# Reordering the end of a mixture-of-experts tail: sixteen small dense blocks, the last expert, and one instruction of each finish

## Chip, cores and metric

The kernel runs on one core of a Trainium2 chip. The metric is device time in microseconds (us), the median of several runs of one whole launch. Engines are named as in the profile: PE (TensorE matmuls), PEld (its weight loads), DVE (VectorE), ACT (ScalarE), POOL (GpSimd), SP (SyncE, which only starts DMAs here).

## What is computed

The input is x of shape (4, 32, 32, 64): four images of 1024 tokens with 64 channels. A Mamba-like mixer (convolution, selective scan, projection) with a residual comes first, then a layer norm and a top-1 mixture of experts:

```
logits = h @ gate_w + gate_b;  probs = softmax(logits);  idx = argmax(probs)
pos  = rank of the token within its expert;  kept = pos < C      # C = 640 slots an expert, 8 experts
buf[idx, pos] = h                                                 # dropped where not kept
hmid = relu(buf @ w1[e] + b1[e]);  ybuf = hmid @ w2[e] + b2[e]    # 64 -> 256 -> 64
y    = nan_to_num(ybuf[idx, pos] * prb * kept, nan=0, posinf=1e4, neginf=-1e4)
out  = t + y                                                      # t: the residual
```

## The kernel before

The program writes out each engine's order of work by hand; engines meet through semaphores. The first three quarters are the mixer: per image and state a scan on DVE, with ACT, POOL and PE around it. The experts come at the end, and the change is there.

**Slots.** All tokens but the last 256 are scattered by their slot number to a table in DRAM (`slots`, eight experts of 640 rows, 5 tiles of 128). The table is read back, one load an expert (`xe[e]`), and worked in 16 chunks: `CHUNKS` holds for each expert a chunk of 3 tiles (384 rows) and one of 2 tiles (256 rows). For chunk i, PE does `turn(i)` (transposes, L1142), ACT `channels(i)` (copy, L878), PE `up(i)` (two matmuls 64 to 256, L1153), ACT `hidden(i)` (two ReLUs, L886 and L888). When both chunks of an expert are there PE does `down` (20 matmul passes for 5 tiles, L1167). `FINISH` lists nine finishes, two for expert 0 and one for each other; so `down(8)` and `finish(8)` are those of the last expert, e=7. `finish(i)` runs on DVE (L1495 to L1509): add the bias, multiply by the gate, replace non-finite numbers, add the residual. POOL then scatters the expert's five tiles to the output rows, one indirect DMA a tile (L615).

**The last 256 tokens** (`LT = 2` tiles) have no time to go through the table. They are computed densely, through all eight experts, with a selector row that shuts the wrong ones: 16 blocks j of half an expert each: PE `dense_up(j)` (L1184), ACT `dense_hidden(j)` (L895), PE `dense_down(j)` (L1196), which all add up in one PSUM bank. Their finish on DVE (L1522 to L1530) is followed by one direct DMA from SP (L454).

**Order at the end.** `BEHIND = 8`: behind each of the last eight chunks PE does one `dense_up` and the `dense_down` of the block before; then `down(8)`; then the other eight blocks in a row:

```
if i >= BEHIND:
    dense_up(i - BEHIND)
...
down(E)
for j in range(len(CHUNKS) - BEHIND, BLOCKS):
    dense_up(j)
    dense_down(j - 1)
dense_down(BLOCKS - 1)
```

On DVE the dense finish comes last, behind `finish(8)`. ACT follows PE's order. POOL ends with `finish(8)`'s five DMAs and a wait for all output scatters; SP ends with the dense tokens' DMA and a wait for it.

Of the kernel before, what the change touches and what calls it, by code (L numbers as in the profile page):

```python
# [5 lines left out]
ALU = mybir.AluOpType  # L6
# [7 lines left out]
B, H, W, C = 4, 32, 32, 64  # L14
# [14 lines left out]
CHUNKS = [(e, k0, k1) for e in range(E) for k0, k1 in ((0, 3), (3, ET))]  # L29
BLOCKS = 2 * E  # L30
FINISH = [(0, 0, 3), (0, 3, ET)] + [(e, 0, ET) for e in range(1, E)]
BEHIND = 8
BAR = 2.0 ** 100
R_RES, R_PRB, R_ID, ROW = C, 2 * C, 2 * C + 1, 2 * C + 2
LT = 2
LW = LT * P
UNITS = [(b, 0, T) for b in range(B - 1)] + [(B - 1, 0, T - LT), (B - 1, T - LT, LT)]
V = len(UNITS)
# [24 lines left out]
def metaformer_layer(nc, x, ln_g, ln_b, in_proj_w, conv_w, conv_b, x_proj_w, dt_proj_w, dt_proj_b, A_log,  # L63
# [7 lines left out]
    with ExitStack() as ctx:  # L71
        def sb(name, shape, dt=F32):
            return ctx.enter_context(nc.sbuf_tensor(name, shape, dt))
# [8 lines left out]
        M0 = ctx.enter_context(nc.psum_tensor("M0", [P, HALF], F32))  # L82
# [77 lines left out]
        bs = sb("bs", [P, 25, T])  # L160
# [18 lines left out]
        def within(buf, start, *dims):  # L179
            size = 1  # L180
            for d in dims:
                size *= d
            flat = buf[:, :, :].rearrange("p a l -> p (a l)")[:, start:start + size]
            names = "abcd"[:len(dims)]
            if len(dims) == 1:
                return flat
            return flat.rearrange(f"p ({' '.join(names)}) -> p {' '.join(names)}",
                                  **{k: d for k, d in zip(names[1:], dims[1:])})
# [10 lines left out]
        ye = within(dA, 0, 4, ET, C)  # L199
# [3 lines left out]
        dy = within(bsb, 2 * L + HALF, 4, LT, C)  # L203
        dout = within(bsb, 3 * L, LT, C)
        dfin = within(bsb, 3 * L + HALF, LT, C).bitcast(I32)

        def four(buf):
# [33 lines left out]
             "b_lgt b_h3 b_ld b_ex b_oh b_base b_acc b_pos b_prb b_ids b_idx b_dve b_dve2 b_dve3 b_res b_sent").split())  # L241

        fill_done, w1_zero, bars = sem("fill_done"), sem("w1_zero"), sem("bars")
        b_hx, d_tr, d_xT, d_up, d_hid, d_dn, d_dve, d_diff, d_fin, d_out = map(
            sem, "b_hx d_tr d_xT d_up d_hid d_dn d_dve d_diff d_fin d_out".split())
        e_in = [sem(f"e_in{e}") for e in range(E)]
        e_out = [sem(f"e_out{i}") for i in range(2)]
        e_zero, e_tr, e_xT, e_up, e_h0, e_h1, e_dn, e_y, e_yo, e_dve, e_diff = map(sem, (
            "e_zero e_tr e_xT e_up e_h0 e_h1 e_dn e_y e_yo e_dve e_diff").split())

        def at(buf, b):

# [9 lines left out]
        def over(col, n):  # L262

            return col.unsqueeze(2).broadcast_to([P, col.shape[1], n])
# [76 lines left out]
        def rows(v):  # L341

            return rows_[:, v % 2]
# [9 lines left out]
        def tiles(psum, n, k=T):  # L353
            return psum.rearrange("p (t c) -> p t c", t=k)[:, :, 0:n]
# [268 lines left out]
        def _(act):  # L623
# [267 lines left out]
            def dense_hidden(j):  # L891
                act.wait_ge(d_up, j + 1)
                if j >= 2:
                    act.wait_ge(d_dn, j - 1)
                ac.activation(hid[:, j % 2, :], Yp[:, j % 2 * HALF:j % 2 * HALF + LW], ACT.Relu,  # L895
                              bias=b1c[:, j:j + 1]).then_inc(d_hid, 1)
# [6 lines left out]
            for i in range(len(CHUNKS)):  # L903
                if 2 <= i + 1 < len(CHUNKS):
                    channels(i + 1)
                hidden(i)
                if i == BEHIND - 1:
                    act.wait_ge(d_tr, 1)
                    ac.activation(hxT[0:HX, :], Yp[0:HX, HALF:HALF + LW], ACT.Copy).then_inc(d_xT, 1)
                if i >= BEHIND:  # L910
                    dense_hidden(i - BEHIND)
            for j in range(len(CHUNKS) - BEHIND, BLOCKS):
                dense_hidden(j)


        @block.tensor
        def _(pe):
# [260 lines left out]
            def dense_up(j):  # L1178
                e, part = j // 2, j % 2
                if j < 2:  # L1180
                    pe.wait_ge(d_xT, 1)
                else:
                    pe.wait_ge(d_hid, j - 1)
                te_.matmul(Yp[:, j % 2 * HALF:j % 2 * HALF + LW], w1s[0:HX, e, part * P:(part + 1) * P], hxT[0:HX, :], start=True,  # L1184
                           stop=True).then_inc(d_up, 1)

            def dense_down(j):
                e, part = j // 2, j % 2
                if j == 0:
                    pe.wait_ge(b_idx, V)  # L1190
                    for t in range(LT):
                        te_.matmul(M0[:, t * C:(t + 1) * C], hxT[0:HX, t * P:(t + 1) * P], b2z[0:HX, :], start=(t == 0),
                                   stop=False, skip_group_check=True)
                pe.wait_ge(d_hid, j + 1)
                for t in range(LT):
                    ins = te_.matmul(M0[:, t * C:(t + 1) * C], hid[:, j % 2, t * P:(t + 1) * P], w2s[:, e, part, :],  # L1196
                                     start=False, stop=(j == BLOCKS - 1 and t == LT - 1), skip_group_check=True)
                ins.then_inc(d_dn, 1)
# [38 lines left out]
            for i in range(len(CHUNKS)):  # L1237
                if i + 1 < len(CHUNKS):
                    turn(i + 1)
                if i == 1:  # L1240
                    down(0)
                up(i)
                if i == 0:
                    back(LAST, 15)
                if i == 1:
                    down(1)
                if i >= 4 and i % 2 == 0:
                    down(i // 2)
                if i == BEHIND - 1:
                    dense_turn()  # L1250
                if i >= BEHIND:
                    dense_up(i - BEHIND)
                if i >= BEHIND + 1:
                    dense_down(i - BEHIND - 1)
            down(E)
            for j in range(len(CHUNKS) - BEHIND, BLOCKS):
                dense_up(j)
                dense_down(j - 1)
            dense_down(BLOCKS - 1)


        @block.vector
        def _(dve):
            ve = nc.vector
# [223 lines left out]
            def finish(i):  # L1488
                e, k0, k1 = FINISH[i]
                m = k1 - k0  # L1490
                link = Chain(dve, e_dve, i, 4)
                y, cl, ok, diff = (ye[:, x, k0:k1] for x in range(4))
                inf = fin[:, k0:k1, :]
                dve.wait_ge(e_dn, i + 1)
                ve.tensor_tensor(y, tiles(turned_down(i), C, m),  # L1495
                                 b2s[:, e, :].unsqueeze(1).broadcast_to([P, m, C]), ALU.add).then_inc(e_y, 1)
                dve.wait_ge(e_y, i + 1)
                link(ve.tensor_tensor(y, y, xe[e][:, k0:k1, R_PRB:R_PRB + 1].broadcast_to([P, m, C]), ALU.mult))

                ve.tensor_tensor(diff, y, y, ALU.subtract).then_inc(e_diff, 1)  # L1500
                ve.tensor_scalar(cl, y, 1e4, -1e4, ALU.min, ALU.max)
                link(ve.tensor_tensor(ok, y, y, ALU.is_equal))
                dve.wait_ge(e_diff, i + 1)
                ve.tensor_scalar(inf, diff, 0.0, None, ALU.is_equal)
                link(ve.tensor_tensor(cl, cl, ok, ALU.mult))
                link(ve.copy_predicated(cl, inf, y))
                if e >= 2:
                    dve.wait_ge(e_out[e % 2], 16 * ET * (e // 2))
                ve.tensor_tensor(yo[:, e % 2, k0:k1], cl, xe[e][:, k0:k1, R_RES:R_RES + C], ALU.add).then_inc(e_yo, 1)  # L1509
                link.end()  # L1510

            finish(0)
            back(LAST, 15)
            for i in range(1, len(FINISH)):
                finish(i)

            link = Chain(dve, d_dve, 0, 4)
            y, cl, ok, diff = (dy[:, i] for i in range(4))
            nt = LT
            dve.wait_ge(d_dn, BLOCKS)  # L1520
            dve.wait_ge(b_idx, V)
            link(ve.tensor_tensor(y, tiles(M0[:, 0:nt * C], C, nt), over(bs[:, 23, 0:nt], C), ALU.mult))  # L1522
            ve.tensor_tensor(diff, y, y, ALU.subtract).then_inc(d_diff, 1)
            ve.tensor_scalar(cl, y, 1e4, -1e4, ALU.min, ALU.max)
            link(ve.tensor_tensor(ok, y, y, ALU.is_equal))
            dve.wait_ge(d_diff, 1)
            ve.tensor_scalar(dfin[:, :, :], diff, 0.0, None, ALU.is_equal)
            link(ve.tensor_tensor(cl, cl, ok, ALU.mult))
            link(ve.copy_predicated(cl, dfin[:, :, :], y))
            ve.tensor_tensor(dout[:, :, :], cl, rows(V - 1)[:, 0:nt, R_RES:R_RES + C], ALU.add).then_inc(d_fin, 1)  # L1530
            link.end()


# [27 lines left out]
```

## Time and profile before

| what | value |
|---|---|
| timed runs | 387.02, 388.14, 391.14 us; median 388.14 us |
| profiled execution, first to last instruction | 397.8 us |
| mean granted TensorE clock of the profiled execution | 0.868 |
| busy share of the span: PE, DVE, POOL, ACT | 79%, 78%, 71%, 59% |

The timed runs and the profiled execution are different executions. No total time of the profiled one stands beside its span; the span alone is 9.7 us longer than the median of the timed runs. A granted clock of 1.00 is 2.4 GHz, 0.50 is 1.2 GHz.

### The profile page before, as it was taken

How to read it: one execution, taken by the hardware profiler on the slowest of the kernel's cores; microseconds unless marked ns; L12 is line 12 of the kernel's file. 1: busy time of each engine (PE TensorE's matmuls, PEld its weight loads, DVE VectorE, ACT ScalarE, POOL GpSimd, SP SyncE). 2: the span in 40 equal slices, each digit the busy share in tenths (PEclk: the TensorE clock that was granted, in tenths of full speed). 3: DMA queues.
4: the chain of work that ended last, by engine and by line, in shares of the span. 5: the costliest groups of instructions: out<-in, count | busy, mean ns of one | idle time of the engine just before them, and what ended most of it. 6: DMA issues, size and time to landing. Idle time of an engine off the chain costs nothing. (4 is left out here: it accounts for less than half of the span.)

```text
span 397.8 us, 4347 instructions
## 1 busy us (share of the span) xinstructions
PE 316.1 (79%) x1257; PEld 188.4 (47%) x1257; DVE 310.1 (78%) x360; ACT 233.3 (59%) x519; POOL 282.1 (71%) x201
## 2 busy tenths in 40 slices
PE   7832986957989896897989698796895798869784
PEld 3311432313535352553545265363773576748764
DVE  4799987999999999987999989999981157425441
ACT  4456797524798984659797268775651455234221
POOL 3435846987993999999599999966877044745760
PEclk9965897999998998879899898989987599968955
DMA  4287999999798699856878769997210900000000
GB/s 99 36 281 248 274 243 366 390 200 368 315 315 323 208 308 297 284 190 244 303 254 298 203 175 325 318 369 226 61 30 19 250 23 4 18 8 17 16 1 8
DMA packets 43986, 78.68 MB, mean 198 GB/s; under 512 B 16050, under 2 KB 26093, under 8 KB 43962
## 3 DMA queue, kind: packets, MB, share of 16 engines
q1 hardware_dynamic: 41066, 73.88, 57.5%
q0 software_dynamic: 2896, 4.53, 4.2%
q8 instruction: 10, 0.16, 0.2%
q14 instruction: 14, 0.11, 0.1%
HBM read 72.30 MB, written 7.54 MB: 201 GB/s over the span
## 5 line engine op out<-in xcount | busy, mean ns | idle before, releaser
L518 POOL TENSOR_TENSOR prod<-h,csb 128x1024 f32<-128x1024 f32 (+1 forms) x64 | 143.7, 2253 | 24.9 <-DMA csb<-bc_rows 10.5
L984 PE MATMUL Yp<-prod,ident 128*128 128x512 f32 (+1 forms) x256 | 124.9, 624 | 13.8 <-POOL prod L518 13.6
L1318 DVE TENSOR_TENSOR_SCAN h<-dA,Bp 128x1024 f32<-128x1024 f32 (+2 forms) x58 | 119.7, 2064 | 4.7 <-DVE Bp L1277 1.0
L984 PEld LDWEIGHTS Yp<-prod,ident 128*128 128x128 f32 x256 | 50.3, 208 | 75.3 <-issue 50.3
L697 ACT ACTIVATE dA<-delta,aneg 128x1024 f32<-128x1024 f32 (+1 forms) x58 | 62.9, 1093 | 23.1 <-DVE h L1318 19.0
L1277 DVE TENSOR_TENSOR Bp<-Cp,bsb 128x1024 f32<-128x1024 f32 (+1 forms) x58 | 67.7, 1168 | 6.4 <-DMA bsb<-bc_rows 4.2
L615 POOL DMA_INDIRECT out_dram<-dA,csb x30 | 30.3, 1009 | 36.5 <-DVE dA L1509 28.9
L558 POOL DMA_INDIRECT slots<-rows_,slot x30 | 30.1, 1002 | 6.9 <-issue 4.5
L1495 DVE TENSOR_TENSOR dA<-Bp,b2s 128x320 f32<-128x320 f32 (+1 forms) x8 | 3.8, 475 | 33.8 <-PE Bp L1167 15.6
L1153 PE MATMUL Cp<-prod,w1s 128*128 128x384 f32 (+1 forms) x64 | 24.7, 508 | 2.0 <-issue 2.0
L895 ACT ACTIVATE bsb<-Yp,b1c 128x256 f32<-128x256 f32 x16 | 7.6, 475 | 23.4 <-PE Yp L1184 14.0
L1167 PEld LDWEIGHTS Bp<-w2s,prod 128*128 128x128 f32 x152 | 18.5, 195 | 2.3 <-issue 1.0
L1167 PE MATMUL Bp<-w2s,prod 128*128 128x64 f32 x152 | 18.3, 276 | 0.2 <-ACT prod L888 0.2
L1196 PEld LDWEIGHTS M<-w2s,bsb 128*128 128x128 f32 x64 | 13.6, 269 | 7.3 <-issue 5.7
L1196 PE MATMUL M<-w2s,bsb 128*128 128x64 f32 x64 | 12.9, 344 | 4.8 <-issue 4.8
L1153 PEld LDWEIGHTS Cp<-prod,w1s 128*128 128x128 f32 x64 | 12.1, 216 | 7.4 <-issue 5.4
L878 ACT ACTIVATE prod<-Bp 64x384 f32<-64x384 f32 (+1 forms) x16 | 6.8, 427 | 14.8 <-PE Bp L1142 7.6
L1184 PE MATMUL Yp<-hxT,w1s 72*128 72x256 f32 x32 | 13.7, 519 | 0.6 <-issue 0.6
L567 POOL TENSOR_TENSOR bsb<-te,bsb 128x1024 f32<-128x1024 f32 (+1 forms) x6 | 13.1, 2179 | 1.2 <-DMA bsb<-bc_rows 1.1
L615 POOL DMA_INDIRECT out_dram<-dA,bsb x10 | 10.1, 1013 | 4.7 <-issue 2.9
L526 POOL TENSOR_TENSOR trel<-trel,ex 128x1024 f32<-128x1024 f32 x3 | 7.1, 2359 | 8.7 <-DVE h L1318 4.9
L886 ACT ACTIVATE prod<-Cp,b1c 128x384 f32<-128x384 f32 (+1 forms) x16 | 8.4, 525 | 7.9 <-PE Cp L1153 5.8
(290 smaller groups left out, 604.8 us busy)
## 6 DMA issues: line engine op xcount, KB each, us to landing
bsb<-bc_rows SPq DMA_DIRECT2D x48, 512.0 KB, 6.7
csb<-bc_rows SPq DMA_DIRECT2D x48, 512.0 KB
bsb<-bc_rows SPq DMA_DIRECT2D x16, 384.0 KB, 5.7
csb<-bc_rows SPq DMA_DIRECT2D x16, 384.0 KB
slots<-fill POOLq DMA_DIRECT2D x1, 2600.0 KB
csb<-slots SPq DMA_DIRECT2D x6, 325.0 KB, 5.3
bcs<-bc_rows SPq DMA_DIRECT2D x2, 512.0 KB, 10.9
xs_in<-in_x_dram SPq DMA_DIRECT2D x1, 768.0 KB, 5.8
```

What stands on the lines that cost most here:

```text
L518: po.tensor_tensor(prod[:, k % 4, c], h[:, k % 3, c], csb[:, k % CSLOTS, c], ALU.mult).then_inc(s_pP, 1)
L558: po.indirect_dma_start(slots_dram[:, :], bass.IndirectOffsetOnAxis(ap=slot[:, v % 2, t:t + 1], axis=0), rows(v)[:, t, :], None, bounds_ch ...
L567: po.tensor_tensor(row, te[:, c], row, ALU.mult).then_inc(p_bx, 1)
L615: po.indirect_dma_start(out_rows, bass.IndirectOffsetOnAxis(ap=xe[e][:, k, R_ID:R_ID + 1].bitcast(I32), axis=0), yo[:, e % 2, k, :], None, ...
L697: ac.activation(dA[:, k % 3, c], at(delta, UNITS[v][0])[:, c], ACT.Exp, scale=aneg[:, n:n + 1]).then_inc(s_dA, 2 if (v, n - 1) in POOLED e ...
L984: ins = te_.matmul(Yp[:, c], idn, prod[:, k % 4, c], start=False, stop=(n == 15), skip_group_check=True)
L1153: te_.matmul(Cp[:, k * HALF:k * HALF + (k1 - k0) * P], w1s[:, e, k * P:(k + 1) * P], xT[:, e % 2, k0 * P:k1 * P], start=True, stop=True).t ...
L1167: ins = te_.matmul(turned_down(i)[:, (k - k0) * C:(k - k0 + 1) * C], part[:, e % 2, k * P:(k + 1) * P], w2s[:, e, x, :], start=(x == 0), s ...
L1184: te_.matmul(Yp[:, j % 2 * HALF:j % 2 * HALF + LW], w1s[0:HX, e, part * P:(part + 1) * P], hxT[0:HX, :], start=True, stop=True).then_inc(d ...
L1196: ins = te_.matmul(M0[:, t * C:(t + 1) * C], hid[:, j % 2, t * P:(t + 1) * P], w2s[:, e, part, :], start=False, stop=(j == BLOCKS - 1 and ...
L1277: ve.tensor_tensor(Bp[:, span(v)], Cp[:, span(v)], bsb[:, k % CSLOTS, span(v)], ALU.mult).then_inc(s_mul, 2 if (v, n - 1) in POOLED else 1)
L1318: ins = ve.tensor_tensor_scan(h[:, k % 3, c], decays, drives, h[:, k % 3, c.start - 1:c.start] if i else 0.0, ALU.mult, ALU.add)
```

## The change

Three edits. First, PE does two dense blocks behind each of the last eight chunks, so all sixteen lie in the loop, and `dense_down(15)` and then `down(8)` come last; ACT's order follows. Second, DVE does the dense finish ahead of `finish(8)`, which is now its last work. Third, in both finishes the test for finite numbers is one instruction, `(y * 0) == 0`, in place of a subtraction `y - y` and a comparison with 0 that waited for it; the semaphores of that wait go.

```diff
 # ACT
                 if i >= BEHIND:
-                    dense_hidden(i - BEHIND)
-            for j in range(len(CHUNKS) - BEHIND, BLOCKS):
-                dense_hidden(j)
+                    dense_hidden(2 * (i - BEHIND))
+                    dense_hidden(2 * (i - BEHIND) + 1)
 # PE
                 if i >= BEHIND:
-                    dense_up(i - BEHIND)
-                if i >= BEHIND + 1:
-                    dense_down(i - BEHIND - 1)
+                    j = 2 * (i - BEHIND)
+                    dense_up(j)
+                    if j:
+                        dense_down(j - 1)
+                    dense_up(j + 1)
+                    dense_down(j)
+            dense_down(BLOCKS - 1)
             down(E)
-            for j in range(len(CHUNKS) - BEHIND, BLOCKS):
-                dense_up(j)
-                dense_down(j - 1)
-            dense_down(BLOCKS - 1)
 # DVE, finish(i); the dense finish likewise, now a function finish_dense()
-                ve.tensor_tensor(diff, y, y, ALU.subtract).then_inc(e_diff, 1)
+                ve.tensor_scalar(inf, y, 0.0, 0.0, ALU.mult, ALU.is_equal)
                 ve.tensor_scalar(cl, y, 1e4, -1e4, ALU.min, ALU.max)
                 link(ve.tensor_tensor(ok, y, y, ALU.is_equal))
-                dve.wait_ge(e_diff, i + 1)
-                ve.tensor_scalar(inf, diff, 0.0, None, ALU.is_equal)
                 link(ve.tensor_tensor(cl, cl, ok, ALU.mult))
 # DVE, order
-            for i in range(1, len(FINISH)):
+            for i in range(1, len(FINISH) - 1):
                 finish(i)
+            finish_dense()
+            finish(len(FINISH) - 1)
```

## Rows read from the trace of the kernel before

**Rows 1.** Stretches of 10 us: busy PE, PEld, DVE, ACT, POOL, granted clock, DMA
```profile
340.00:350.00 10.00, 7.90 (x51) 6.54 (x49) 4.08 (x9) 2.51 (x6) 7.56 (x9) 1.00 0.06 21
360.00:370.00 10.00, 10.00 (x70) 8.91 (x70) 4.25 (x10) 4.26 (x9) 7.01 (x7) 0.95 0.05 18
380.00:390.00 10.00, 8.55 (x31) 7.33 (x30) 2.00 (x5) 2.85 (x6) 5.94 (x6) 0.50 0.02 1
```

**Rows 2.** Chain of waits, last expert at full clock (start, us, what)
```profile
362.97 0.49 PE Yp L1184 x2
...
369.56 0.49 PE Yp L1184 x2
370.04 0.39 PE M L1196 x4
...
371.36 0.43 PE Yp L1184 x2
```

**Rows 3.** Chain of waits, dense blocks behind the last expert
```profile
374.42 0.49 PE Yp L1184 x2
...
375.78 2.65 issue
...
380.51 1.45 issue
...
388.19 0.96 PE Yp L1184 x2
389.15 0.75 PE M L1196 x4
...
390.86 1.69 PE M L1196 x8
```

**Rows 4.** Timeline: dense finish on DVE, first and last, and its DMA
```profile
392.57 0.29 DVE L1522 TENSOR_TENSOR bsb<-M,bs 128x128 f32<-128x128 f32 x1 [10.47 <-PE M L1196]
...
394.36 0.29 DVE L1530 TENSOR_TENSOR bsb<-bsb,rows_ 128x128 f32<-128x128 f32 x1
394.67 0.38 SPq L454 DMA_DIRECT2D out_dram<-bsb  x1
```

**Rows 5.** Timeline: finish of expert 6 on DVE
```profile
369.59 0.49 DVE L1495 TENSOR_TENSOR dA<-Bp,b2s 128x320 f32<-128x320 f32 x1 [2.57 <-PE Bp L1167]
...
370.64 0.49 DVE L1500 TENSOR_TENSOR dA<-dA 128x320 f32<-128x320 f32 x1
...
371.06 0.55 DVE L1501 TENSOR_SCALAR dA<-dA 128x320 f32<-128x320 f32 x1
...
371.53 0.47 DVE L1502 TENSOR_TENSOR dA<-dA 128x320 f32<-128x320 f32 x1
...
372.04 0.33 DVE L1504 TENSOR_SCALAR dA<-dA 128x320 int32<-128x320 f32 x1
372.28 0.48 DVE L1505 TENSOR_TENSOR dA<-dA 128x320 f32<-128x320 f32 x1
...
373.35 0.49 DVE L1509 TENSOR_TENSOR dA<-dA,bsb 128x320 f32<-128x320 f32 x1
```

**Rows 6.** Timeline: POOL's DMAs of experts 6 and 7, first and last of five
```profile
374.63 0.97 POOL L615 DMA_INDIRECT out_dram<-dA,bsb  x1 [0.50 <-issue]
...
380.03 1.09 POOL L615 DMA_INDIRECT out_dram<-dA,bsb  x1 [0.30 <-issue]
...
382.90 0.97 POOL L615 DMA_INDIRECT out_dram<-dA,bsb  x1 [1.78 <-DVE dA L1509]
...
388.00 0.97 POOL L615 DMA_INDIRECT out_dram<-dA,bsb  x1 [0.30 <-issue]
```

**Rows 7.** Chain of waits: an indirect DMA of POOL, from issue to landing
```profile
306.38 2.19 DMA slots<-rows_,slot
```

**Rows 8.** Timeline: work that waited for PE in two stretches
```profile
345.43 2.34 PE L1167 MATMUL Bp<-w2s,prod 128*128 128x64 f32 x20
...
355.63 0.49 DVE L1495 TENSOR_TENSOR dA<-Bp,b2s 128x320 f32<-128x320 f32 x1 [10.84 <-remote]
...
377.86 0.49 DVE L1495 TENSOR_TENSOR dA<-Bp,b2s 128x320 f32<-128x320 f32 x1 [4.02 <-remote]
377.90 0.47 ACT L895 ACTIVATE bsb<-Yp,b1c 128x256 f32<-128x256 f32 x1 [5.60 <-issue]
```

**Rows 9.** Stretches of 2 us, columns as in rows 1
```profile
376.00:378.00 2.00, 0.00 (x0) 0.00 (x0) 0.14 (x1) 0.10 (x1) 1.70 (x2) 1.00 0.06 18
378.00:380.00 2.00, 1.57 (x6) 1.35 (x6) 1.93 (x5) 0.38 (x1) 1.42 (x2) 0.51 0.01 0
...
386.00:388.00 2.00, 2.00 (x10) 1.82 (x9) 0.00 (x0) 0.72 (x2) 1.39 (x2) 0.50 0.01 0
```

More of the change, by code:

```diff
@@ L243, in metaformer_layer @@
         fill_done, w1_zero, bars = sem("fill_done"), sem("w1_zero"), sem("bars")
-        b_hx, d_tr, d_xT, d_up, d_hid, d_dn, d_dve, d_diff, d_fin, d_out = map(
-            sem, "b_hx d_tr d_xT d_up d_hid d_dn d_dve d_diff d_fin d_out".split())
+        b_hx, d_tr, d_xT, d_up, d_hid, d_dn, d_dve, d_fin, d_out = map(
+            sem, "b_hx d_tr d_xT d_up d_hid d_dn d_dve d_fin d_out".split())
         e_in = [sem(f"e_in{e}") for e in range(E)]
         e_out = [sem(f"e_out{i}") for i in range(2)]
-        e_zero, e_tr, e_xT, e_up, e_h0, e_h1, e_dn, e_y, e_yo, e_dve, e_diff = map(sem, (
-            "e_zero e_tr e_xT e_up e_h0 e_h1 e_dn e_y e_yo e_dve e_diff").split())
+        e_zero, e_tr, e_xT, e_up, e_h0, e_h1, e_dn, e_y, e_yo, e_dve = map(sem, (
+            "e_zero e_tr e_xT e_up e_h0 e_h1 e_dn e_y e_yo e_dve").split())
         def at(buf, b):
@@ L1491, in finish @@
                 link = Chain(dve, e_dve, i, 4)
-                y, cl, ok, diff = (ye[:, x, k0:k1] for x in range(4))
+                y, cl, ok = (ye[:, x, k0:k1] for x in range(3))
                 inf = fin[:, k0:k1, :]
@@ L1510, in finish, with finish_dense @@
                 link.end()
+            def finish_dense():
+                link = Chain(dve, d_dve, 0, 4)
+                y, cl, ok = (dy[:, i] for i in range(3))
+                nt = LT
+                dve.wait_ge(d_dn, BLOCKS)
+                dve.wait_ge(b_idx, V)
+                link(ve.tensor_tensor(y, tiles(M0[:, 0:nt * C], C, nt), over(bs[:, 23, 0:nt], C), ALU.mult))
+                ve.tensor_scalar(dfin[:, :, :], y, 0.0, 0.0, ALU.mult, ALU.is_equal)
+                ve.tensor_scalar(cl, y, 1e4, -1e4, ALU.min, ALU.max)
+                link(ve.tensor_tensor(ok, y, y, ALU.is_equal))
+                link(ve.tensor_tensor(cl, cl, ok, ALU.mult))
+                link(ve.copy_predicated(cl, dfin[:, :, :], y))
+                ve.tensor_tensor(dout[:, :, :], cl, rows(V - 1)[:, 0:nt, R_RES:R_RES + C], ALU.add).then_inc(d_fin, 1)
+                link.end()
             finish(0)
             back(LAST, 15)
-            for i in range(1, len(FINISH)):
+            for i in range(1, len(FINISH) - 1):
                 finish(i)
[L1517 to L1531, printed above, removed]
+            finish_dense()
+            finish(len(FINISH) - 1)
 _INS = ['x', 'L0_conv_ln_g', 'L0_conv_ln_b', 'L0_conv_in_proj_w', 'L0_conv_conv_w', 'L0_conv_conv_b',
```

## Prediction

> **What bounds the kernel now.** I read the table of stretches first, since the change touches only the last 60 us, then the chain of waits through the end, and then the timeline of each engine that finishes something there. In the table the reader is to see that PE limits the stage where the slot experts and the dense blocks are mixed: from 360 to 370 it is busy for 10.00 of 10.00 us while DVE, ACT and POOL have room [rows 1]. The chain agrees: from the end of `down(6)` to the end of `down(7)`, 362.97 to 369.56, it stays on PE throughout, 6.59 us for an expert with two dense blocks [rows 2]. Behind `down(8)`, which ends at 374.42, the chain is still PE's: eight dense ups and nine downs until 392.55, 18.13 us, of which 4.10 (2.65 and 1.45) are waiting without a visible cause and the rest is work, most of it at the half clock [rows 3]. Then come the dense finish and its DMA: 392.57 to 394.67 on DVE, and from there to the end of the span at 397.8 another 3.13 [rows 4]. In all, 23.4 us from the end of `down(8)` to the end.
>
> A second way ends beside it and is almost hidden in this trace: `finish(8)` on DVE and POOL's five indirect DMAs, the last issued at 388.00 [rows 6]. With about 2.2 us to land [rows 7] that was done near 390.2, some 7 us ahead of the dense way. So the question is which of the two ways is the longer one when the dense blocks run faster than here.
>
> **The profiled execution and the timed ones.** The span is 397.8 us and the median of the timed runs 388.14, so the profiled execution lost at least 9.7 us that the timed runs did not lose. I looked in the chain for losses that no instruction explains, and found two stretches where signals from PE come late. PE's record of `down(5)` ends at 345.43 + 2.34 = 347.77, but DVE, which waits for it, starts at 355.63; `down(6)` ends 15.2 us after `down(5)` where 6.59 is the pace, so this stretch cost 8.6 us. In the second, DVE's `finish(8)` starts at 377.86 and ACT's next dense ReLU at 377.90, though PE put half a microsecond of work between the two signals [rows 3, 8]: two signals that should lie 0.49 apart arrive 0.04 apart, as if they had been held back together. PE had then nothing to do from 376 to 378, and its granted clock fell from 1.00 to 0.51 in the next 2 us [rows 9]. Without the late signal I see no reason for the fall. I take it that the timed runs have neither, in the main; that is the choice on which the forecast hangs, and the rivals are its other outcomes.
>
> The Trainium skill has two rules that bear on it, and the sum below doesn't use them. TensorE: Matmul & The Clock Gate (Part 1) says that the half clock is the state of rest and that sustained activity releases it; by that a tail of back-to-back dense blocks would run at the full clock, as I take it, though the trace speaks against it for a while: PE is busy for 2.00 of 2.00 us from 386 to 388 at a granted 0.50 [rows 9]. Runtime: NRT & Kernel Launch (The launch sequence) gives 9 to 15 us around the instructions of a kernel; if the timed runs hold that, their span would be an estimated 373 to 379 us, and more than the 9.7 us of late signals and half clock would be missing from them; no run here shows it.
>
> **The change, part by part.** All times from D, the end of `down(8)` in the old order, at the full clock and without late signals.
>
> Before, dense way: 8 ups at 0.43 to 0.49 and 9 downs at 0.39 make 3.7 + 3.5 = 7.2 us [rows 2], then 392.55 to 397.8, 5.25 [rows 4]: D + 12.5. At the half clock the ups cost 0.96 and the downs 0.75, 14.4 us [rows 3]: D + 19.7.
>
> Before, POOL way: it starts with expert 6. `down(7)` ends 4.86 us ahead of D (369.56, 374.42). `finish(7)` runs from 369.59 to 373.84, 4.25 us, and POOL's first DMA comes 0.79 later, at 374.63 [rows 5, 6]; that is 5.07 behind `down(7)`. Its five DMAs hold POOL from 374.63 to 381.12, 6.49; then 0.3 of issue, and expert 7's five, 382.90 to 388.97, 6.07. Expert 7's result is ready sooner (4.86 + 5.07 = 9.93 behind `down(7)`) than POOL is free (11.9). The last DMA lands 2.19 after its issue, 1.22 after the end of its record, and the close of the program takes about 0.4 (the span's end less 394.67 and the direct DMA's median of 2.7). Sum: 5.07 + 6.49 + 0.3 + 6.07 + 1.22 + 0.4 = 19.55 behind `down(7)`, or D + 14.7. This is longer than the dense way's 12.5: where PE is not slowed, the end of the kernel before is POOL's.
>
> After, PE: the eight blocks move ahead of `down(8)`. They fill no hole, since PE had none in that stage at the full clock [rows 1, 2]; the stage gets longer by what they cost, and `down(8)` ends at D + 7.2. In the loop the order up(j), down(j-1), up(j+1), down(j) leaves 0.39 + 0.43 = 0.8 us between an up and the down that needs its ReLU of 0.47 [rows 2, 8], so I charge nothing for waits; behind `hidden` of the same chunk ACT is some 0.6 us late, and if that cover went the cost would be up to 0.3 a chunk, 2.4 in all (the upper bound).
>
> After, DVE: `finish_dense` is queued ahead of `finish(8)`. It waits for `dense_down(15)`, which ends a `down` (2.2 us) before `finish(8)` can start, and takes about 2.1 less one instruction [rows 4]: covered. SP's DMA of the dense tokens goes out sooner and is off the path; nothing else is queued on SP. POOL is free again: `finish(7)` is now some 7 us ahead of `finish(8)` and not 4.9.
>
> The shorter finish: the steps from L1500 to L1505 took 372.28 - 370.64 = 1.64 us for four instructions. Three are left, of which the new two-operation one is bounded by the starts of its kind: 0.24 (L1504 to L1505) and 0.47 (L1501 to L1502) [rows 5]. So 0.2 to 0.4 us is saved in each finish; I take 0.2, since the new one has two operations as L1501. Only the last one lies on the path; the others are covered by PE's 6.6 to 8.3 us an expert.
>
> After, the end: behind `down(8)` come `finish(8)` 0.03 + 4.05, the step to POOL 0.79, five DMAs 6.07, landing 1.22, close 0.4: 12.6 us, with no way round it. End: D + 7.2 + 12.6 = D + 19.8.
>
> **Sum.** +5.1 us against D + 14.7: 388.14 + 5.1 = 393.2 us. What is moved behind the common PE work is the longer finish (12.6 us against the dense 5.25), and the POOL time that used to run beside the dense blocks now has nothing beside it. Bounds of this case: POOL's five at 6.07 or 6.49, the saved 0.2 or 0.4, PE's waits 0 to 2.4, and POOL's lag before: 3.9 to 7.5, or 392 to 395.6.
>
> Against the profiled execution the same end would be 374.42 + 19.8 = 394.2, 3.6 us shorter than 397.8, because that one paid 4.1 of late signals and 7 of half clock behind D.
>
> **Rivals.** *The tail of the timed runs is at the half clock, without late signals* (chance 0.20). For it: the clock did not come back in 18 us of dense blocks [rows 3, 9]. Then before ends at D + 19.7 by the dense way, and after, whose blocks lie among chunks that ran at 1.00, at D + 19.8: 388.2.
>
> *The timed runs are like the profiled one and the new order mends it* (0.17), the case on the other side: before ends at D + 23.4, and PE, with two blocks and the next chunk at hand, bridges the late signals; after at D + 19.8 is 3.6 us faster, 384.5, and if it bridges part of the first stretch's 8.6 too, down to 380. It decides from the point where late signals and half clock cost the timed tail more than 5.1 us. Against it: 9.7 us of span that the timed runs don't have.
>
> *The new loop itself is slowed* (0.10): four dense blocks an expert with more hand-overs between PE and ACT bring a wait that drops the clock. One expert with four blocks takes 6.59 + 2 x 0.85 = 8.3 us at the full clock and twice that at half; one such expert gives +8.3: 401.5.
>
> *The change does nothing* (0.03): the end of the timed runs is set by something that neither order moves: 388.
>
> **How the numbers follow.** The first case has 0.50. Runs of one kernel here differ by 1% (387.02 to 391.14), so within 1% means 384.3 to 392.0. Slower by over 1%: 0.43 of the first case and 0.10 of the slowed loop, 0.53. Within 1%: 0.07 of the first, 0.20, 0.03 and a little of the third, 0.32 together. Faster by over 1%: 0.15 from the third. The range runs from 384.3 to 397: below it some 0.1 of the third case is left out, above it the slowed loop.
>
> **What will show it.** Right: in the profile of the changed kernel the chain ends with `down`'s L1167, the DVE finish, five POOL DMAs at L615 and a landing, about 12.6 us behind the last matmul; SP's dense DMA lands more than 8 us before the end; an expert with four dense blocks takes about 8.3 us at full clock, with PE busy all the time. Wrong: gaps of PE in the last eight chunks that the second block fills (an expert with four blocks at less than 7.5 us), or a timed gain, which would say that the timed runs before had the half clock or the late signals behind `down(8)`; or DVE's L1495 starting well behind the last L1167.

## Result and profile after

The changed kernel takes 390.63 us (median of 20 runs, 387.46 to 398.71), the kernel before 388.79 us (20 runs, 384.58 to 395.87). Their ratio is 1.0071, 95% interval 1.0038 to 1.0104: 1.5 to 4.0 us slower, 2.8 at the middle. Some executions of either kernel take some per cent longer at a lower granted clock; the ratios leave them out and the medians do not, so a ratio is not the quotient of two medians. The profiled execution of the changed kernel took 393.05 us, 1.85 us more than its span of 391.2; so a time and a span differ by little here.

The chain of waits at the end of the changed kernel (start, us, what):

```profile
369.27 0.50 PE Yp L1183 x2
...
370.98 2.25 PE Bp L1166 x20
...
373.25 0.50 DVE dA L1494
...
376.37 0.50 DVE dA L1506
...
382.77 0.97 POOL out_dram L615
```

The way is the one that was forecast: the last down of PE, the last finish on DVE, five DMAs of POOL. The last matmul ends at 373.23, and 18.0 us follow, against the 5.25 that followed the last matmul in the first profile of the kernel before [rows 4]. The five-us stretches of the same kernel (columns as in rows 1) show the stage itself:

```profile
345.00:350.00 5.00, 5.00 (x37) 4.42 (x37) 0.86 (x2) 2.42 (x5) 3.78 (x5) 1.00 0.09 30
360.00:365.00 5.00, 5.00 (x35) 4.30 (x34) 1.01 (x2) 3.33 (x8) 3.48 (x4) 1.00 0.07 23
365.00:370.00 5.00, 5.00 (x35) 4.62 (x34) 3.44 (x8) 2.49 (x6) 2.41 (x3) 1.00 0.05 12
```

PE is busy throughout at the full clock; an expert with four dense blocks takes 8.35 us (the dense ups behind one expert's down start at 349.07, 357.42 and 365.77 in the chain). But POOL, busy 3.78 us of 5 when it issues one DMA after the other, falls to 2.41: it runs dry. Its timeline in the changed kernel, the first DMAs of experts 5, 6 and 7 and the last of all:

```profile
361.87 0.97 POOL L615 DMA_INDIRECT out_dram<-dA,csb  x1 [0.91 <-DVE dA L1506]
...
370.21 0.97 POOL L615 DMA_INDIRECT out_dram<-dA,bsb  x1 [2.19 <-DVE dA L1506]
...
377.66 0.97 POOL L615 DMA_INDIRECT out_dram<-dA,bsb  x1 [1.02 <-DVE dA L1506]
...
382.77 0.97 POOL L615 DMA_INDIRECT out_dram<-dA,bsb  x1 [0.31 <-issue]
```

The brackets give POOL's idle time ahead of each DMA. The comparison is with a second profile of the kernel before, which the first experiment brought (span 382.6; its own time 384.30). It has no late signals and no half clock in this stage, and is called undisturbed below:

```profile
329.72 0.97 POOL L615 DMA_INDIRECT out_dram<-dA,csb  x1 [4.15 <-DVE dA L1509]
...
357.40 2.40 PE L1167 MATMUL Bp<-w2s,prod 128*128 128x64 f32 x20
...
362.52 1.09 POOL L615 DMA_INDIRECT out_dram<-dA,bsb  x1 [0.31 <-issue]
...
367.00 0.66 PE L1196 MATMUL M<-w2s,bsb 128*128 128x64 f32 x4 [0.17 <-ACT bsb L895]
...
369.03 0.97 POOL L615 DMA_INDIRECT out_dram<-dA,bsb  x1 [0.30 <-issue]
...
369.81 0.38 SPq L454 DMA_DIRECT2D out_dram<-bsb  x1
...
374.13 0.97 POOL L615 DMA_INDIRECT out_dram<-dA,bsb  x1 [0.30 <-issue]
```

From expert 1's first DMA at 329.72 on, POOL never waits for DVE again: 35 DMAs, 0.30 apart. The last `down` ends at 359.80, the last matmul at 367.66, the dense tokens' DMA starts at 369.81, and POOL is busy with its DMAs until 375.10. So before, POOL's queue was the end of the kernel, and PE's dense blocks ran beside it at no cost. In this profile 14.9 us follow the last matmul. The spans of the two profiles differ by 8.6 us, but 5.2 of these lie ahead of expert 1's first DMA (329.72, 334.93), where PE's order is the same in both.

In both kernels 7.5 us follow POOL's last record (375.10 to 382.6, 383.74 to 391.2). The trace holds what fills it, though the views leave it out: the landing, and then a drain record on POOL of 5.88 us, from 376.47 in the kernel before and 385.13 in the changed one.

### The profile page after: what moved, and what is told of

It reads as the page before. It is cut to its first block and busy times, and to the rows that moved or that the text cites. A ratio compares the mean times of both kernels' runs of the same rounds, so it can differ in the third digit from the quotient of the medians.

```text
span 391.2 us, 4327 instructions
## 1 busy us (share of the span) xinstructions
PE 305.6 (78%) x1257; PEld 182.0 (47%) x1257; DVE 308.7 (79%) x350; ACT 233.8 (60%) x519; POOL 280.9 (72%) x201
## 5 line engine op out<-in xcount | busy, mean ns | idle before, releaser
L615 POOL DMA_INDIRECT out_dram<-dA,csb x30 | 30.0, 1001 | 28.2 <-DVE dA L1506 20.6
L558 POOL DMA_INDIRECT slots<-rows_,slot x30 | 30.1, 1004 | 6.4 <-issue 5.1
L1152 PE MATMUL Cp<-prod,w1s 128*128 128x384 f32 (+1 forms) x64 | 21.4, 458 | 0.0
L707 ACT ACTIVATE Bp<-delta,aneg 128x512 f32<-128x512 f32 (+1 forms) x12 | 7.8, 652 | 8.4 <-DVE h L1317 8.2
L962 PE MATMUL M<-u,wdt 128*128 128x512 f32 x12 | 8.4, 793 | 4.4 <-ACT u L647 3.2
L691 ACT ACTIVATE Cp<-te 128x1024 f32<-128x1024 f32 x3 | 3.1, 1029 | 14.0 <-DVE Bp L1276 14.0
L1296 DVE TENSOR_TENSOR_SCAN h<-dA,hl,Bp 128x256 f32<-128x256 f32 x16 | 11.0, 731 | 0.3
```

The lines of the kernel that those rows point to most:

```text
L558: po.indirect_dma_start(slots_dram[:, :], bass.IndirectOffsetOnAxis(ap=slot[:, v % 2, t:t + 1], axis=0), rows(v)[:, t, :], None, bounds_ch ...
L615: po.indirect_dma_start(out_rows, bass.IndirectOffsetOnAxis(ap=xe[e][:, k, R_ID:R_ID + 1].bitcast(I32), axis=0), yo[:, e % 2, k, :], None, ...
L1152: te_.matmul(Cp[:, k * HALF:k * HALF + (k1 - k0) * P], w1s[:, e, k * P:(k + 1) * P], xT[:, e % 2, k0 * P:k1 * P], start=True, stop=True).t ...
L1296: ve.tensor_tensor_scan(h[:, ring(q), w], dA[:, ring(q), w], Bp[:, w], hl[:, n:n + 1], ALU.mult, ALU.add).then_inc(s_scan, 1)
```

## Experiments

The theory, call it A: POOL's 35 DMAs from expert 1 to the end take about 45 us without a gap, plus 7.5; the kernel's end moves by the gaps that an order of PE leaves in that queue, and by nothing else. Rivals: the loss lies in PE's longer loop, in the clock, in the new finish, or the kernel before lost time in a slow dense tail. Whole times of one kernel scatter by some per cent, and much of that arises ahead of the stage changed here: in the twelve later profiles POOL's first DMA of expert 0 starts anywhere from 319.5 to 324.9. So beside each ratio stands the *tail*: from POOL's first DMA of expert 1 to the end of the span, in the one profile of each kernel, and POOL's idle time in it beyond the 0.31 between two DMAs. Each ratio is against the kernel before in the same rounds.

| kernel | ratio to before (95%) | tail, us | POOL idle, us |
|---|---|---|---|
| before, again | 1.0011 (0.9962 to 1.0060) | 52.86 | 0.0 |
| changed | 1.0071 (1.0038 to 1.0104) | 56.31 | 3.2 |
| order alone | 1.0118 (1.0036 to 1.0200) | 56.29 | 4.0 |
| finish alone | 1.0052 (1.0001 to 1.0103) | 53.40 | 0.0 |
| all blocks last | 0.9982 (0.9942 to 1.0022) | 53.03 | 0.0 |
| twelve in the loop | 1.0030 (0.9992 to 1.0068) | 53.84 | 1.3 |
| changed, last expert in two | 1.0071 (1.0031 to 1.0111) | 55.32 | 2.5 |
| changed, SP waits | 1.0067 (1.0022 to 1.0111) | 54.91 | 2.8 |
| before, SP waits | 0.9953 (0.9912 to 0.9994) | 51.49 | 0.0 |
| before, finish and SP waits | 0.9979 (0.9945 to 1.0014) | 52.03 | 0.0 |
| before, by chunks | 0.9850 (0.9779 to 0.9921) | 51.13 | 0.0 |

**Before, again** (no edit).

> The kernel before, unchanged, for a second profile. Theory A (the late signals and the half clock of the first profile are not the rule): the span is 385 to 388 us, no wait of DVE for PE behind a finished down is longer than 2 us, and POOL's last DMA and the drain behind it (5.9 us in both profiles) end within 2 us of the dense tokens' DMA. Rival R (they are the rule): two late stretches again, 8 and 4 us, and the end 23 us behind the last expert's down, by the dense way alone.

The late signals did not come again and the clock was full until the last matmul, as A expected; the span, 382.6, was 2.4 us under the range named. The dense tokens' DMA and POOL's end were not within 2 us of each other: that DMA started 5.3 us ahead of the end of POOL's last DMA and 12.5 ahead of the end of the drain, so POOL's way was the longer one by more than expected.

**Order alone and finish alone.** The changed kernel with the old finish, and the kernel before with the new one (both edits as in the diff above).

> The order of after with the old finish. Theory A: the order carries the whole loss, 0.2 to 0.6 us above after, ratio to before 1.007 to 1.010. Rival (the new finish costs, the order is free): the time of before, ratio 1.000.

> The order of before, only the finish with one instruction less. Theory A: 0.2 to 0.6 us less, ratio 0.998 to 1.000, since one finish at most lies on the path. Rival (DVE's finishes pace the last experts): eight finishes at 0.4 to 0.6 us, 3 to 5 us less, ratio 0.988 to 0.992.

The order carries the loss: its tail is the changed kernel's (56.29 and 56.31), and not 0.2 to 0.6 us above it as expected. Its gaps are 0.8 us longer than the changed kernel's, but its 35 DMAs hold POOL 0.7 us less (34.4 and 35.2). So A's "by nothing else" holds to about half a microsecond: in the kernels of the table the 35 DMAs take between 34.4 and 35.6 us of POOL's time. The finish alone gains nothing; its interval lies at or above 1, and its tail is 0.54 longer although POOL has no gap. The cost is in POOL's DMAs themselves, summed over experts 0 to 5 and 6 to 7; first before, then with the new finish (busy, mean ns):

```profile
L615 POOL DMA_INDIRECT out_dram<-dA,csb x30 | 30.0, 1001 | 28.0 <-DVE dA L1509 19.8 <-issue 8.2
L615 POOL DMA_INDIRECT out_dram<-dA,bsb x10 | 9.8, 984 | 3.0 <-issue 3.0
```

```profile
L615 POOL DMA_INDIRECT out_dram<-dA,csb x30 | 30.5, 1017 | 27.7 <-DVE dA L1507 20.7 <-issue 7.0
L615 POOL DMA_INDIRECT out_dram<-dA,bsb x10 | 9.9, 990 | 3.0 <-issue 3.0
```

The same 0.5 us lies between the two kernels with SP's wait (51.49 and 52.03). The expected small gain did not come; what came is a loss of that size, in one profile of each.

**Without the last expert's DMAs** (changed kernel; 640 rows of the output are not written).

```diff
-                for k in range(k0, k1):
+                for k in range(k0, k1 if e < E - 1 else k0):
...
-                pool.wait_ge(e_out[i], 16 * ET * len(range(i, E, 2)))
+                pool.wait_ge(e_out[i], 16 * ET * len(range(i, E - 1, 2)))
```

> After, without the last expert's five output DMAs (its 640 rows are not written). Theory A (the end is POOL's way: five DMAs, a landing, then a drain of 5.9 us): the drain starts behind expert 6's landing, so the end comes some 7 us sooner, span near 384. Rival (the drain or the end waits for PE, DVE or SP): less than 2 us, or, if the drain shrinks when little is outstanding, 13 us or more.

The span is 383.7, 7.5 us less than the changed kernel's, though PE and DVE end where they did (373.17 and 376.81, there 373.22 and 376.87). POOL's five DMAs are the end, not the finish. This is one execution, without a ratio. The drain took 5.47 us with five DMAs fewer, 0.41 less. Two values don't tell how much of it is fixed: at 0.08 us a DMA, an estimate from these two, the 40 output DMAs would make 3.3 of the 5.88, and with the 30 that POOL issues to fill the table (L558) nearly all of it.

**Where the wait stands.** The wait for the output's landing goes from POOL to SP, in the kernel before and in the changed one.

```diff
 # POOL
-            for i in range(2):
-                pool.wait_ge(e_out[i], 16 * ET * len(range(i, E, 2)))
 # SP, at its end
+            for i in range(2):
+                sp.wait_ge(e_out[i], 16 * ET * len(range(i, E, 2)))
```

> The order and the finish of before; only the wait for the output DMAs' landing goes from POOL to SP, so POOL's drain can start at once behind its last DMA. Theory A (POOL's way ends the kernel, and the drain is a fixed 5.5 to 5.9 us that needn't wait for the landing): 1.2 us less in the end, ratio 0.997. Rival (the drain waits for the landing itself, or the dense way is the end): no change; the drain is 1.2 us longer.

> After, with the same one edit. Theory A: 1.2 us less than after, ratio to before 1.004 to 1.006. Rival: as after, 1.007.

Both tails are 1.4 us shorter (52.86 to 51.49, 56.31 to 54.91), and POOL's last record now lies 6.1 us ahead of the end in place of 7.5: the landing goes on beside the drain. That the same edit is worth the same in both shows that POOL's way ends both kernels. The ratio of the kernel before (0.9953) agrees; that of the changed one (1.0067 beside 1.0071, where 1.004 to 1.006 was expected) is too coarse to show it.

**Last expert in two parts** (changed kernel).

```diff
-FINISH = [(0, 0, 3), (0, 3, ET)] + [(e, 0, ET) for e in range(1, E)]
+FINISH = [(0, 0, 3), (0, 3, ET)] + [(e, 0, ET) for e in range(1, E - 1)] + [(E - 1, 0, 3), (E - 1, 3, ET)]
...
-                done = i + 1 if i < 2 else 2 * e + 2
+                done = 2 * e + (1 if k1 == 3 else 2)
...
                     if j:
                         dense_down(j - 1)
+                    if i == len(CHUNKS) - 1:
+                        down(E)
                     dense_up(j + 1)
...
-            down(E)
+            down(E + 1)
```

> After, with the last expert finished in two parts: three tiles in the middle of the last chunk, two at the very end. Theory A (the loss is POOL standing idle while PE does the dense blocks ahead of the last down): POOL starts on the last expert sooner and has only two DMAs behind the last down, so 3 to 4.5 us come back, ratio to before 0.997 to 1.002, the gaps between POOL's experts but the last two unchanged. Rival (the loss is in PE's longer loop or in the clock): as after, 1.007, or worse for a finish more on DVE.

POOL's timeline in it, the first DMAs of experts 5 and 6, the first of expert 7 and the last:

```profile
361.77 0.97 POOL L615 DMA_INDIRECT out_dram<-dA,csb  x1 [0.92 <-DVE dA L1508]
...
370.10 0.97 POOL L615 DMA_INDIRECT out_dram<-dA,bsb  x1 [2.18 <-DVE dA L1508]
...
376.57 0.97 POOL L615 DMA_INDIRECT out_dram<-dA,bsb  x1 [0.30 <-issue]
...
381.67 0.97 POOL L615 DMA_INDIRECT out_dram<-dA,bsb  x1 [0.30 <-issue]
```

The tail fell by 1.0 us, not by 3 to 4.5. The number was worked out against A's own rule: POOL is held by expert 6's DMAs until 376.3 whenever they started at 370.1, so only the last gap of 1.02, less the 0.31 of issue, could go. The gaps at 361.77 and 370.10 are as in the changed kernel, as A wants. The ratio is too coarse to tell 1 us.

**All blocks last, and twelve in the loop.** In the kernel before, `BEHIND = 16` puts all sixteen dense blocks behind the last expert; the other edit puts two blocks behind each of chunks 8 to 11, one behind each of 12 to 15, four behind the last expert.

> Before, with all sixteen dense blocks behind the last expert and none in the loop. Theory A (POOL paces the end, PE's order is free as long as POOL is fed): POOL has no gap from the second expert on, the end is POOL's drain, the time of before to 0.5%. Rival (the dense blocks alone at the end run at the half clock and end last): sixteen blocks at 1.7 us, PE's last matmul some 10 us later than in the second profile of before, the end 5 to 8 us later.

> The finish and the DVE order of before; twelve dense blocks in the loop, two behind each of chunks 8 to 11 and one behind each of the last four, four behind the last expert. Theory A (an expert with four dense blocks takes PE 8.35 us and POOL 6.4, so each lets POOL run dry by up to 2 us once its queue is used up): of two such experts the queue of 3 to 4 us covers nearly all, POOL's gaps together 0 to 1 us, ratio 1.000 to 1.003. Rival (any block ahead of the last down costs its 0.85 us): 3.4 us later, ratio 1.009.

With all blocks last PE ends later against POOL's queue, and nothing is lost: no gap, a tail of 53.03. These blocks, 14 us of dense work in a row, ran at the full clock (five-us stretches of that kernel):

```profile
360.00:365.00 5.00, 5.00 (x37) 4.58 (x36) 2.45 (x7) 2.69 (x6) 3.78 (x4) 1.00 0.06 19
365.00:370.00 5.00, 5.00 (x36) 4.49 (x36) 0.49 (x1) 2.56 (x7) 3.78 (x5) 1.00 0.03 7
```

That ends the rival of a dense tail at the half clock for the executions that were profiled. Here the queue even holds DVE back: the last expert's finish waits 4.25 us for expert 5's rows to land before it may write over them in one of the two output buffers:

```profile
366.81 0.49 DVE L1510 TENSOR_TENSOR dA<-dA,bsb 128x320 f32<-128x320 f32 x1 [4.25 <-DMA out_dram<-dA,csb]
```

With twelve in the loop there is one large gap in the queue beyond expert 1, where the pairs have used it up, and a small one of 0.50 ahead of expert 6:

```profile
361.93 0.97 POOL L616 DMA_INDIRECT out_dram<-dA,csb  x1 [1.43 <-DVE dA L1510]
```

Idle 1.3 us, a little over the 0 to 1 expected; the tail is 1.0 longer than before's. The rival's 0.85 us for each block moved would have given 3.4. So 0, 8, 12 and 16 blocks ahead of the last down, all with the old finish, give tails of 53.0, 52.9, 53.8 and 56.3: no price until POOL's queue is empty.

**Before, with the new finish and SP's wait; then by chunks.** If POOL's queue is the end, it ends sooner when it is fed sooner. So every chunk gets a down and a finish of its own:

```diff
-FINISH = [(0, 0, 3), (0, 3, ET)] + [(e, 0, ET) for e in range(1, E)]
+FINISH = CHUNKS
 # ACT, hidden
-                    act.wait_ge(e_dn, e)
+                    act.wait_ge(e_dn, 2 * (e - 1))
 # PE
-                done = i + 1 if i < 2 else 2 * e + 2
+                done = i + 1
...
-                if i >= 4 and i % 2 == 0:
-                    down(i // 2)
+                if i >= 3:
+                    down(i - 1)
...
-            down(E)
+            down(len(CHUNKS) - 1)
```

> The order of before, with the shorter finish and the wait for landings on SP. Theory A (POOL, fed without a gap from expert 1 on, sets the end; a shorter finish only makes its queue longer): 1.3 us less by SP's wait and nothing by the finish, ratio 0.995 to 0.998. Rival (the finish counts too): a further 0.5 us or more.

> As finish_sp, with every chunk finished by itself (16 finishes of 3 or 2 tiles in place of 9), each chunk's down behind the next chunk's up. Theory A (POOL can end sooner only if it is fed sooner): the gap of 5.1 us ahead of expert 1 shrinks to under 3.5, the rest of the queue stays closed, the end comes 2 to 4 us sooner still, ratio to before 0.987 to 0.993. Rival (DVE, with 16 finishes, falls behind, and opens new gaps): no gain over finish_sp, gaps of POOL spread over the experts.

POOL's timeline by chunks, the first DMA of expert 0, the first of expert 1 and the last:

```profile
323.19 0.96 POOL L617 DMA_INDIRECT out_dram<-dA,csb  x1 [15.77 <-DVE dA L1507]
...
329.79 0.97 POOL L617 DMA_INDIRECT out_dram<-dA,csb  x1 [0.36 <-issue]
...
373.84 0.97 POOL L617 DMA_INDIRECT out_dram<-dA,bsb  x1 [0.30 <-issue]
```

With the new finish and SP's wait alone the ratio is 0.9979, within the range expected but not clear of 1. By chunks, the gap ahead of expert 1 (4.15 in the undisturbed profile, 5.17 in the first) is down to 0.36, and no other opened. From expert 0's first DMA to the end it takes 57.7 us (323.19 to 380.9) where the kernel before takes 63.1 (319.51 to 382.6); 1.4 of these 5.4 us are SP's wait. The ratio is 0.985 (0.978 to 0.992), medians 381.78 (6 runs) and 385.93: this version is faster than the kernel before, and so than the changed one, which was not timed beside it. DVE did not fall behind.

## Why the prediction came out as it did

The likeliest case was right in its sign and its mechanism: the eight blocks fill no hole of PE, which was busy in 5.00 of 5.00 us; they push the last `down` back; the finish that ends last is followed by five DMAs of POOL, and before, POOL's way and not the dense one was the end. Its size was too large: +5.1 us forecast with bounds of 3.9 to 7.5; 2.8 (1.5 to 4.0) measured, 3.45 by the tails. At +0.7% the result is among the outcomes within 1%, to which the prediction gave 0.32, and not among those slower by over 1%, which had 0.53.

The term that was mis-sized is POOL's lag before. The sum let POOL's way start with expert 6, its first DMA 5.07 us behind `down(7)`, and so expert 7's DMAs 7.0 us behind D (5.07 + 6.49 + 0.3, less 4.86). In the undisturbed profile expert 6's start 7.6 us behind `down(7)`, and expert 7's at 369.03, 9.2 us behind D at 359.80. DVE's finish of an expert starts as its `down` ends. Its starts there for experts 2, 3 and 6, and POOL's first DMA of expert 3 between them:

```profile
330.03 0.49 DVE L1495 TENSOR_TENSOR dA<-Bp,b2s 128x320 f32<-128x320 f32 x1 [1.10 <-PE Bp L1167]
...
335.15 0.49 DVE L1495 TENSOR_TENSOR dA<-Bp,b2s 128x320 f32<-128x320 f32 x1 [1.04 <-PE Bp L1167]
...
342.49 1.17 POOL L615 DMA_INDIRECT out_dram<-dA,csb  x1 [0.30 <-issue]
...
354.97 0.49 DVE L1495 TENSOR_TENSOR dA<-Bp,b2s 128x320 f32<-128x320 f32 x1 [2.33 <-PE Bp L1167]
```

Experts without dense blocks leave PE every 5.12 us, while five DMAs at a pitch of 1.28 take 6.4. So POOL's first DMA of an expert comes 0.8 us behind the end of DVE's finish for expert 1, but 2.0 and 3.3 for experts 2 and 3; it stays there for 4 to 6, whose two dense blocks make PE about as slow as POOL. The first profile, from which the sum was read, hid this: its first late signal had emptied the queue.

```profile
360.44 0.97 POOL L615 DMA_INDIRECT out_dram<-dA,csb  x1 [6.94 <-DVE dA L1509]
```

Both paces stood in that profile, so the lag could have been worked out. The queue's slack was larger than the sum had it and covered more of the delay: 16 blocks ahead of the last `down` cost POOL 3.2 us of idle time, not 5.

The other terms, from the two profiles. Eight blocks: 7.2 forecast, 7.9 measured behind D (359.80 to 367.66). The last finish and the step to POOL: 4.87 forecast, 4.44 measured (373.22 to 377.66). Its five DMAs: 6.07 and 6.08. Landing and close: 1.6 forecast, 7.5 measured; the drain of POOL was missed because no view lists it. In the first profile it ran from 390.35 to 396.23, so POOL's way ended there some 1.6 us ahead of the span's end and not the 7 us that the prediction read. That it stands at the end of both kernels, so that the difference did not suffer, is luck; the two absolute ends did suffer (D + 14.7 was D + 22.8, and D + 19.8 was D + 25.9). So the measured terms make 3.1 us in place of 5.1: the lag took 2.2 away, the blocks added 0.7, and the finish took 0.4. It also changes the first rival: with the drain POOL's way before is longer than a dense tail at the half clock, D + 19.7, so by these numbers that rival would have given the same loss, and not 388.2.

The choice on which the forecast hung, that late signals and the half clock are not the rule, held: the twelve later profiles, the changed kernel's and eleven experiments', have the full clock from expert 0's DMAs until PE's last matmul, and in none does PE's signal reach DVE late. With 1.85 us around it the first profiled execution would have taken 399.65, more than each of the 20 runs of before; in a later round one of 35 runs of before took 399.59, so an execution that long is rare and not unique, and no trace shows what that one holds. What held PE's signals back in the first profile stays open. The Trainium skill's page TensorE: Matmul & The Clock Gate (Part 1) says that sustained activity releases the half clock. The 14 us of dense blocks at 1.00 don't speak against it, but they came in at 1.00 and so show that the clock was kept, not released; in the first profile it stayed at 0.50 from 380 to 390 with PE busy for 8.55 us [rows 1]. The Trainium skill's page Runtime: NRT & Kernel Launch (The launch sequence) gives 9 to 15 us around a kernel's instructions. Outside the span this metric has 1.7 to 1.9 us in each run, so what the prediction estimated by that page, timed spans of 373 to 379 us, is not the case.

The rival on the other side and the slowed loop did not occur: PE's pace with four blocks was 8.35 us against 8.3 worked out. The shorter finish was counted as a gain of 0.2. DVE's last finish did get shorter by 0.5 (359.83 to 363.93 before, 373.25 to 376.87 after), but alone it measured as no gain, since before POOL's queue is the end.

## What to carry to other kernels

Where one engine issues the stores of everything at a fixed pace, write down when each of its inputs is ready against when it is free: here, what was moved ahead of an input cost nothing until that queue was empty, and the rest of the delay afterwards. A tail that ends on a long fixed way (here 18 us of finish, five DMAs, landing and drain) belongs behind as little as possible, and a short one (here 5) can go last. Feeding the queue sooner, by finishing smaller pieces, gave more here than any order tried of the work in front of it.

## Hardware, not expected

POOL's closing drain took 5.88 us with 40 output DMAs and 5.47 with 35; it ended 5.9 us after POOL's last DMA even where it was issued with DMAs still in front of it (SP's wait), so a wait for landings ahead of it is paid on top: 7.5 us from POOL's last DMA to the end in place of 6.1. An indirect DMA of POOL took 0.97 us in most cases and up to 1.29 (the changed kernel with SP's wait); in the four profiles of before again, changed, order alone and finish alone, all 28 that took over 1.00 us ran beside a compute instruction of DVE. The mean over experts 0 to 5 rose from 1001 to 1017 ns when the finish was changed; which of DVE's instructions does that was not tried by itself.
